# Max pass: GpSimd makes a small copy of its own and waits for it between the gathers of two chunks

## What is computed

```python
Wd, Ws, ww = (Wm[:H], Wm[H:2 * H], Wm[2 * H])
msgs = z[edge_dst] @ Wd + z[edge_src] @ Ws + edge_weight[:, None] * ww[None, :] + bm
agg = jax.ops.segment_max(msgs, edge_dst, num_segments=n)
hidden = jax.nn.relu(z @ W1a + agg @ W1b + b1)
return hidden @ W2 + b2
```

## Time and profile before

| what | value |
|---|---|
| median of 3 runs | 3882.38 us (3880.49 to 3886.64) |
| span of the profiled execution | 3851.9 us |
| GpSimd's gathers of the max pass | 1961.35 to 3186.3 us of the span |
| mean granted TensorE clock, whole span | 0.818 of full speed |

### The profile page before, as it was taken

The page is one execution under the profiler, slowest core; times in us unless marked ns, Lnnn a source line. Parts: engine busy times, 40 slices in busy tenths (PEclk is TensorE's granted clock), DMA queues, the critical chain, the costliest instruction groups (busy, mean ns, idle before and its releaser), DMA issues.

```text
span 3851.9 us, 54329 instructions
## 1 busy us (share of the span) xinstructions
PE 3125.2 (81%) x21070; PEld 2150.6 (56%) x21070; DVE 1459.7 (38%) x3223; ACT 958.7 (25%) x2512; POOL 2340.9 (61%) x2327
## 2 busy tenths in 40 slices
PE   3788788878889888888857787878878787999898
PEld 2444444455557677777735555555656564555454
DVE  6555555223222111111224444544444443333333
ACT  2555455122222011010122222322222232000000
POOL 3666662666662665666446666666666662777775
PEclk7899999899999999999955665665665667999899
DMA  5444444655555666666433343433444337666564
GB/s 150 162 160 166 167 149 156 200 175 185 190 181 172 193 193 188 198 193 201 144 112 103 108 116 101 119 102 112 112 127 127 111 113 253 211 226 218 195 225 144
DMA packets 278767, 621.83 MB, mean 161 GB/s; under 512 B 60077, under 2 KB 188649, under 8 KB 270953
## 3 DMA queue, kind: packets, MB, share of 16 engines
q1 hardware_dynamic: 171944, 372.56, 28.5%
q0 software_dynamic: 104832, 244.47, 22.5%
q10 hardware_dynamic: 1728, 1.25, 0.1%
HBM read 477.62 MB, written 140.45 MB: 160 GB/s over the span
## 4 chain that ended last, share of the span: by engine, by line
PE 56%; another core or an unknown queue 15%; issue 13%; DVE 7%; ACT 6%; DMA 3%; SPq 1%; DVEq 0%; POOL 0%; ACTq 0%; POOLq 0%
PE banks L2056 27%; PE banks L1294 5%; PE banks L2077 4%; PE banks L554 3%; PE banks L2075 3%; PE banks L1283 3%; PE banks L1272 3%; PE banks L1274 1%; PE banks L529 1%; PE banks L2170 1%; PE banks L1154 1%; DMA ring_of_rows<-weight_parts 1%; ACT arena L2363 1%; ACT arena L1213 1%
## 5 line engine op out<-in xcount | busy, mean ns | idle before, releaser
L2056 PE MATMUL banks<-arena 128*128 128x384 bf16 (+1 forms) x9310 | 1557.1, 316 | 129.0 <-issue 114.3
L2056 PEld LDWEIGHTS banks<-arena 128*128 128x128 bf16 x9310 | 914.4, 100 | 618.0 <-issue 235.8
L516 POOL DMA_INDIRECT arena<-tab_l,ring_of_rows x831 | 808.4, 973 | 472.3 <-issue 286.3
L2121 POOL DMA_INDIRECT arena<-h_pieces,span_sources x450 | 435.8, 968 | 319.2 <-issue 108.3
L2121 POOL DMA_INDIRECT ring_of_rows<-message_pieces,span_sources x396 | 430.2, 1086 | 214.1 <-issue 98.0
L2121 POOL DMA_INDIRECT ring_of_rows<-x_pieces,span_sources x306 | 332.9, 1088 | 201.3 <-PE banks L2075 101.1
L1294 PE MATMUL banks<-arena 128*128 128x64 f32 x1662 | 349.8, 380 | 123.4 <-issue 123.0
L2101 DVE TENSOR_TENSOR arena<-iota_bf,span_targets 128x768 bf16<-128x768 bf16 x243 | 134.9, 556 | 822.3 <-remote 318.3
L2121 POOL DMA_INDIRECT ring_of_rows<-l_pieces,span_sources x306 | 300.7, 983 | 233.0 <-issue 71.8
L1294 PEld LDWEIGHTS banks<-arena 128*128 128x128 f32 x1662 | 315.9, 284 | 201.5 <-issue 190.4
L1388 DVE TENSOR_TENSOR_SCAN ring_of_rows<-arena,ring_of_rows,banks 128x512 f32<-128x512 bf16 x207 | 264.2, 1277 | 135.6 <-remote 57.7
(11 more groups left out here) (243 smaller groups left out, 3098.4 us busy)
## 6 DMA issues: line engine op xcount, KB each, us to landing
arena<-edge_counts SPq DMA_DIRECT2D x83, 896.0 KB
arena<-edge_counts SPq DMA_DIRECT2D x83, 672.0 KB
edge_counts<-arena SPq DMA_DIRECT2D x32, 1568.0 KB
typed_counts<-arena SPq DMA_DIRECT2D x27, 1568.0 KB
arena<-scan_mask SPq DMA_DIRECT2D x208, 128.0 KB
arena<-typed_counts SPq DMA_DIRECT2D x27, 896.0 KB
arena<-typed_counts SPq DMA_DIRECT2D x27, 672.0 KB
arena<-tab_l,ring_of_rows POOLq DMA_INDIRECT x831
```

The lines of the kernel that those rows point to most:

```text
L516: k.nc.gpsimd.indirect_dma_start(k.RG3[:, i % p.ring, at:at + width], None, table, bass.IndirectOffsetOnAxis(ap=k.SRC[:, i:i + 1], axis=0) ...
L2056: t = T.matmul(k.bank[i % N_SUMS][:, 0:rows.shape[-1]], counts[:, s, :], rows, start=s == 0 and n == 0, stop=s == NT - 1 and n == len(term ...
L2121: G.indirect_dma_start(k.rows[p.layer][s % n], None, k.pieces[p.layer], bass.IndirectOffsetOnAxis(ap=k.SRCG[:, at:at + 1], axis=0)).then_i ...
```

## The change

After the fourth gather of each chunk GpSimd copies the identity matrix into a tensor of its own that nothing reads, and waits on a semaphore that this copy raises. The last chunk has only three gathers and gets none, so there are 207 copies and 207 waits. The new tensor takes 512 bytes in each partition. All other programs are unchanged.

```diff
--- before.py
+++ after.py
@@ -1484,6 +1484,9 @@
         if i >= AHEAD and i % CH == 0:
             G.wait_ge(k.sem("l2_turned"), (i - AHEAD) // CH + 1)
         gather(k, p, i, k.tab["l2"], H, UP)
+        if i % CH == CH - 1:
+            G.tensor_copy(k.BETWEEN, k.IDENT).then_inc(k.sem("l2_between"), 1)
+            G.wait_ge(k.sem("l2_between"), i // CH + 1)
 
 
 def max_sync_l2(k, p):
@@ -3531,6 +3534,7 @@
         k.HT = sb("ht", [P, GMAX * H2])
         k.JUNK = sb("junk", [P, JUNKS, H2], BF16)
         k.FLAG = sb("irregular", [1, 1], I32)
+        k.BETWEEN = sb("between_chunks", [P, P])[:]
         k.IDB, k.IOTAB, k.IOTAB1 = (sb(n, [P, P], BF16)[:] for n in ("identity_bf16", "iota_bf16", "second_iota_bf16"))
         k.one_eps = sb("one_plus_eps", [P, 1])
```

## The result

The changed kernel takes 3908.93 us (median of 4 runs, 3897.35 to 3914.96), the kernel before 3882.05 (4 runs, 3880.49 to 3886.64). The ratio is 1.0059, with a 95% interval of 1.0041 to 1.0077: about 27 us more, where the sum said 2.5. The time lies in the range, but not in the case that was held likeliest.

A forecast was written before the change was run, and what follows sets the result against it. TensorE was taken to bound the max pass, with GpSimd waiting for it. Cover 0, start 1.5 and VectorE 1 gave +2.5 us, added to the median 3882.38 for 3885 us; range 3873 to 3925.

The forecast's parts named there:

- the case that was held likeliest: Whole kernel: a chunk costs GpSimd 0 to 0.81 us, hidden in waits, so time stays the same; chance 0.66.
- The cost of a chunk on GpSimd: Between two chunks' gathers: copy plus wait for it add 0.5 us a chunk, 0.33 to 0.88.
- The cover: Max pass: GpSimd's 167.6 us of waits for TensorE, 0.81 us a chunk, hide the added 104 us.
- The start: First chunks of the max pass: GpSimd has no lead yet, so three copies add 1.5 us, 0 to 2.6.
- VectorE: Max pass: copies and VectorE instructions hold each other up, adding 1 us, bounds 0 and 62.
- rival C: Max pass: GpSimd and VectorE hold each other up on the path, up to 62 us; with a longer start, 0.08.
- 30.5 us around the span: Outside the profiled span: the runs' median of 3882.38 us exceeds the 3851.9 us span by 30.5, which stays.
- Rival A: GpSimd in the max pass: changing between arithmetic and gathers costs 0.76 us more a chunk, +84 us, 3966; chance 0.16.
- Rival B: GpSimd in the max pass: code is loaded anew at each change of kind, 637 us, 4519; chance 0.02.
- Rival D: DMA in the max pass: spaced gathers leave engines to small loads, up to 29 us faster, 3853; chance 0.08.
- The signs I had named: Changed profile: 207 copies of 0.30 us, gaps 0.6 to 0.9, waits about 1, last gather some 11 us ahead.
- S: Follow-up theory, first gather of a chunk: a second wait puts l2_turned's into its own instruction, and that costs; 1.003 to 1.007.

The follow-up runs named there:

- the late wait: Changed kernel with the wait for each copy moved to just ahead of the next chunk's copy: 3855.69 us, 1.0005 against the kernel before; 1.0133 on a faster chip.
- the memsets: Changed kernel with a memset of the same tensor in place of each copy, immediate wait kept: 3876.16 us, 1.0059 against the kernel before.
- the allocation alone: Kernel before with the new tensor made but unused, no copy and no wait: 3848.20 us, 0.9987 against the kernel before.

## Why the prediction missed, step by step

The time lies within the range, but by luck. The part of the range above some 3890 us stood there for chunks that cost GpSimd more than 0.81 us, for VectorE or for a longer start. The loss came at 0.27 us a chunk, by a way that no rival named. The likeliest case, no change, missed at this step:

- **The copy:** 0.299 us at the median, taken as 0.30. Right.
- **The cost of a chunk on GpSimd:** taken as 0.5 (0.33 to 0.88), measured 0.27 at a plain boundary. It is below my low end, because the 0.30 us ahead of a gather do not stay beside the copy: the copy takes their place and only 0.27 follow it. My reason to exclude this, that the gap stands ahead of each gather anyway, was wrong.
- **The cover:** 167.6 us of waits, so nothing on the path. Its first half is shown: the late wait adds the same 66.1 us of copies and costs nothing (1.0005). The half that failed is "the next pair starts when TensorE releases it, as now". With the immediate wait it starts 0.74 us after the update, not 0.26. This is the term that was missing from the sum: 0.48 us at some 66 places, 31 us, of which the passes show 20 to 30. I had costed the added wait by what it does to GpSimd (0.03 to 0.28 us, hidden) and not by what it does to the other wait on the same gather, which is the one that the path runs through.
- **Its bound below the threshold:** the claim that any cost under 0.81 us a chunk is free was not true for where it sits. Of two kernels with 0.47 us, one was free and one was not.
- **The start,** +1.5 us: the first stretch is too short to be told from the spread, and no run isolates it.
- **VectorE,** +1 us, and rival C: VectorE is held 26 times, 2.6 us in all, and the late wait, which holds it 24 times, costs nothing. So the term was right in size, and C falls. The Trainium skill ("SBUF — State Buffer", section "Who interferes with whom") says that a VectorE instruction with two inputs in SBUF and a GpSimd one that reads SBUF exclude each other, and one that only writes doesn't. By that rule the trace agrees, on both: the copies reach 720 ns, the memsets 232. But when VectorE is the one that waits, it is 0.16 us at most, less than a copy's length. The sum that I gave by that rule, 68 us, took every copy to meet one; about 20 of 207 do.
- **30.5 us around the span:** wrong. In the changed kernel's profiled run they are 4.4, and 4.5 with the allocation alone (3848.02 against a span of 3843.5). With as little around it, the profiled execution of the earlier trace rows took about 3856 us, some 26 less than the timed runs. So the difference lies between executions, not around a span; whether that execution ran on the same chip is not on record. The forecast didn't suffer, as I added the sum to the median.
- **Rival A,** a changed kind of work: the first gather after a copy takes 0.97 us, not 1.71. **Rival B,** reloaded code: no gather of the pass takes over 2.7 us. Both fall.
- **Rival D:** the waits for weight_parts after 2012 us on L1274 fall from 12.4 to 8.6 us. Too small to see in the time.
- **The signs I had named:** 207 copies of 0.30 us, yes. A boundary of 0.6 to 0.9 us, slightly less. TensorE waiting for gathered rows once (0.7 us) after 2012 us, in place of never. The last gather ends 8.5 us ahead of the last turning (3222.9 and 3231.4), in place of 11.9. Waits of 1 us, no: they grew. This last sign points at the failed step.

What is shown and what isn't: that the immediate wait makes the loss on the first kind of chip, and not the copy's length, its reads, its tensor or GpSimd's time, is shown by four kernels on one chip. That it does so because the gather starts 0.48 us later behind TensorE's update rests on the traces of six kernels and fits in size. It was not isolated: the kernels made for that (a second wait without a copy; an own wait at another place) ran only where TensorE's updates find no gather waiting. So S is argued from the traces. O, a cost of the own wait itself, is not tested, though the copy had long ended.

## What to carry over

Before you call an added wait hidden, look at which instruction will carry it and what else that instruction waits for. As far as these traces go, the wait that sets the pace should stay alone on its instruction. One's own completion can be collected a round later, here at no cost on the slower chip (1.0005) and with 46.5 in place of 67.3 us on the faster. And slack that a trace shows belongs to that chip: the same GpSimd with 0.81 us to spare for each chunk on one had none on two others.

## What was unexpected

**Chips differ in when TensorE's updates come.** In the kernel before, each recorded update of l2_turned comes 1.8 us (median) after the end of the last L1274 ahead of it, and 2.0 us with the allocation alone; one in ten comes over 5.7 and 6.4 us after. The recorded updates of VectorE and ScalarE come 0.01 us after the end. An example is in the changed kernel's timeline above: L1274 ends at 2606.87 and its update comes at 2610.68, 3.8 us later; those of L1294 and L1283, which ended at 2608.77 and 2609.62, follow at 2610.78 and 2610.84. Such bunches, at least three updates of TensorE, each within 0.12 us of the one before, come some 70 times in the pass of the kernel before and some 50 times in the changed kernel's. Each of them falls into a pause of GpSimd, though its pauses of over 0.35 us fill less than a fifth of the pass. On the two other chips there is no such bunch, and the updates of L1274 come 0.01 us after its end.

The traces of the first kind are also incomplete. In the pass of the kernel before 772 of 871 updates of TensorE are on record and 751 of 1337 of VectorE and ScalarE, and in the changed kernel 39 of the 207 of GpSimd's copies; on the other chips nearly all are. So the exact lateness is uncertain. That it is real in part shows in the gathers, which start 0.26 us behind the recorded update at 93 of 95 waits.

So on the first kind GpSimd's gathers and TensorE's updates are tied to each other, and the pass, 1241 to 1249 us in place of 1090, probably pays for it. That is 151 to 159 of the some 490 us between the kinds of chip; most of the rest lies before the pass, which starts at 1961 us and there at 1680. What ties them, and what differs in the chips, no run shows.
